# Score matmuls of the node slots in three bursts instead of four, the exponent scores first, on one ring of three bank pairs

## What is computed

```
for c in range(6):                       # nodes[-1] is the layer's input
    q = ew[c,0] * (nodes[in_q] @ We[eq] + be[eq])
    k = ew[c,1] * (nodes[in_k] @ We[ek] + be[ek])
    v = ew[c,2] * (nodes[in_v] @ We[ev] + be[ev])
    attn = softmax(heads(q @ Wq[c]) @ heads(k @ Wk[c]).T / sqrt(16))
    nodes[c] = act_w[c] * (attn @ heads(v @ Wv[c])) @ Wo[c] + q
out = layernorm(nodes[5])
```

## Time and profile before

| | |
|---|---|
| median of 3 runs | 1158.76 us (1156.9 to 1162.1) |
| profiled execution: its time, its span | 1160.02 us, 1158.2 us |
| mean granted clock of TensorE | 0.987 of full speed |
| busy share of PE, DVE, ACT, POOL | 96%, 72%, 64%, 37% |
| weight loads (PEld) | 67% |

### The profile page before, as it was taken

One profiled execution on the slowest core, in us unless ns is written; L12 is line 12 of the kernel. 1 busy time (PEld: TensorE's weight loads), 2 busy tenths in 40 slices (PEclk: granted clock), 3 DMA queues, 4 the chain that ended last, 5 costly groups with the idle time before them and its releaser, 6 DMA issues.

```text
span 1158.2 us, 28158 instructions
## 1 busy us (share of the span) xinstructions
PE 1114.4 (96%) x10313; PEld 774.3 (67%) x10313; DVE 836.6 (72%) x1857; ACT 738.9 (64%) x1597; POOL 428.4 (37%) x848
## 2 busy tenths in 40 slices
PE   8989999988999999999999999999999999999995
PEld 3755555555777777777777777677777777777773
DVE  5467888767787777777777788777777777777783
ACT  3345665553666766676666677666766766666674
POOL 3211121123333333333333488533333333333475
PEclk9789999999999999999999999999999999999998
DMA  8000000027665666666666676766666656666540
GB/s 226 1 1 1 1 0 0 1 36 97 91 84 84 93 93 93 86 87 96 93 90 84 87 101 102 104 93 86 88 96 93 90 84 94 94 92 86 84 72 24
DMA packets 83549, 87.02 MB, mean 75 GB/s; under 512 B 11482, under 2 KB 69342, under 8 KB 83422
## 3 DMA queue, kind: packets, MB, share of 16 engines
q1 hardware_dynamic: 81774, 83.17, 49.5%
q0 software_dynamic: 848, 2.11, 1.1%
q10 hardware_dynamic: 800, 0.05, 0.0%
HBM read 6.51 MB, written 2.10 MB: 7 GB/s over the span
## 4 chain that ended last, share of the span: by engine, by line
PE 79%; POOL 6%; DVE 6%; issue 4%; ACT 3%; DMA 1%; ACTq 0%; SPq 0%; POOLq 0%; DVEq 0%
PE bank L1166 71%; PE bank L1519 3%; PE bank L1526 3%; PE bank L1492 1%; DVE region L958 1%; POOL hl L542 1%; POOL region L530 1%; DVE region L992 1%; DMA cols<-in_L_attn_gnorm_w 1%; DVE region L1079 1%; POOL out L600 1%; POOL region L427 1%; POOL xall L429 1%; POOL region L425 1%; POOL region L525 1%
## 5 line engine op out<-in xcount | busy, mean ns | idle before, releaser
L755 ACT ACTIVATE region<-bank 128x512 f32<-128x512 f32 x768 | 416.9, 595 | 262.3 <-PE bank L1166 250.2
L1079 DVE TENSOR_REDUCE region<-bank 128x2 f32<-128x512 f32 x768 | 491.9, 681 | 78.4 <-PE bank L1166 78.1
L1166 PE MATMUL bank<-st 48*128 48x256 f32 x3072 | 374.4, 351 | 2.5 <-DVE region L1079 1.7
L1166 PEld LDWEIGHTS bank<-st 48*128 48x128 f32 x3072 | 265.7, 189 | 81.2 <-issue 29.7
L1166 PE MATMUL bank<-region 128*32 128x256 f32 (+5 forms) x3586 | 256.9, 376 | 2.9 <-DVE region L918 1.1
L542 POOL TENSOR_TENSOR hl<-qk,one_col 128x512 fp32r<-128x512 f32 x96 | 99.9, 1040 | 404.9 <-ACT qk L720 404.9
L1166 PEld LDWEIGHTS bank<-region 128*32 128x32 f32 (+3 forms) x3586 | 129.1, 114 | 90.9 <-issue 23.2
L1166 PE MATMUL bank<-mst,ones 64*128 64x512 bf16 x768 | 150.6, 388 | 0.2 <-ACT region L755 0.2
L545 POOL TENSOR_TENSOR hl<-qk,hl 128x512 fp32r<-128x512 f32 x96 | 122.6, 1277 | 7.5
L1095 DVE COPY mrows<-bank 24x256 bf16<-24x256 bf16 x96 | 26.8, 279 | 98.7 <-PE bank L1492 98.5
L1087 DVE COPY region<-bank 128x512 f32<-128x512 f32 x96 | 64.2, 669 | 2.7 <-PE bank L1166 2.7
(11 more groups left out here) (196 smaller groups left out, 1451.5 us busy)
## 6 DMA issues: line engine op xcount, KB each, us to landing
st<-hl SPq DMA_DIRECT2D x576, 128.0 KB, 4.5
mst<-mrows SPq DMA_DIRECT2D x192, 6.0 KB
out<-xall POOLq DMA_DIRECT2D x15, 128.0 KB, 3.8
xall<-in_L_attn_hidden_states SPq DMA_DIRECT2D x1, 768.0 KB, 8.9
cst<-in_constants SPq DMA_DIRECT2D x1, 514.5 KB, 4.1
xT<-in_L_ffn_Wq SPq DMA_DIRECT2D x1, 384.0 KB
xT<-in_L_ffn_Wk SPq DMA_DIRECT2D x1, 384.0 KB
xT<-in_L_ffn_Wv SPq DMA_DIRECT2D x1, 384.0 KB
```

What stands on the lines that cost most here:

```text
L755: act.activation(to, x_bank(x, k, e)[:, :].rearrange("p (j q) -> p j q", j=2), ACT.Exp).then_inc(B["exp_ok"], 1)
L1079: dve.tensor_reduce(mx[s.n % 2][:, to:to + 2], s_bank(s, k, e)[:, :].rearrange("p (j k) -> p j k", j=2), AX_X, ALU.max, negate=True).then_ ...
L1166: return pe.matmul(o, w, x, start=start, stop=stop, skip_group_check=skip)
```

## The change

PE issues the score work of a slot in three bursts: weights(0), scores(0), scores(1); then weights(1), weights(2), scores(2); then weights(3), scores(3). Both kinds draw bank pairs from one ring of three, and `banks_free` waits for whoever held the pair three places before. `project_v` moves up to where `project_qk` stood, and `project_qk` moves down behind `transpose_ctx`. On DVE `maxes(s, 1)` goes ahead of `copy_rows` and `maxes(s, 2)` ahead of `normalise`. On ACT `copy_vals` follows `exps(x, 2)`, `exps(x, 3)` is cut around `copy_ctxT`, and `copy_qk` comes last. On POOL `split_maxima` works on the step whose maxima have just been taken, at the end of the slot instead of at the start of the next, ahead of `split(a)` and behind the final layer norm.

```diff
-S_RING, X_RING = (0, 1, 2), (4, 5, 6)
+FIRST_RING = (0, 1, 2)
+RING = ((4, 5), (0, 1), (2, 6))
+ORDER = (("x", 0), ("s", 0), ("s", 1), ("x", 1), ("x", 2), ("s", 2), ("x", 3), ("s", 3))
...
 # POOL
             def phase(t, a, s, m, x, d, z, w):
-                if m is not None:
-                    split_maxima(m)
...
+                if s is not None:
+                    split_maxima(s)
                 if a is not None:
                     split(a)
...
 # ACT
+                if x is not None:
+                    exps(x, 2)
+                if m is not None:
+                    copy_vals(m)
                 if z is not None and z.last:
                     inverse_root(fve, fr, z.f, "fve_ok", "frl", "fra", B)
+                if x is not None:
+                    exps(x, 3, (0,))
+                if d is not None:
+                    copy_ctxT(d)
+                if x is not None:
+                    exps(x, 3, (1,))
                 if a is not None:
                     copy_qk(a)
-                if x is not None:
-                    exps(x, 2)
-                if d is not None:
-                    copy_ctxT(d)
-                if m is not None:
-                    copy_vals(m)
-                if x is not None:
-                    exps(x, 3)
...
 # DVE
+                if s is not None:
+                    maxes(s, 1)
                 if m is not None:
                     copy_rows(m)
                 if d is not None:
                     copy_raw(d)
                 if s is not None:
-                    maxes(s, 1)
+                    maxes(s, 2)
                 if d is not None:
                     normalise(d)
                 if s is not None:
-                    maxes(s, 2)
                     maxes(s, 3)
...
 # PE
+            def banks_free(t, kind, k, e):
+                old = holder(place(t, kind, k))
+                if old is None and t == EARLY:
+                    pe.wait_ge(B["max_ok"], UNITS)
+                elif old is None:
+                    pe.wait_ge(A["x1_ok"], ITERS)
+                elif old[0] == "s":
+                    pe.wait_ge(B["max_ok"], old[1] + e + 1)
+                else:
+                    pe.wait_ge(B["exp_ok"], old[1] + e + 1)
...
-                burst(0)
+                burst((0,), (0, 1))
...
-                burst(1)
+                burst((1, 2), (2,))
...
-                if a is not None:
-                    project_qk(a)
+                if m is not None:
+                    project_v(m)
                 if d is not None:
                     transpose_raw(d)
-                burst(2)
+                burst((3,), (3,))
...
                 if d is not None:
                     transpose_ctx(d)
-                if m is not None:
-                    project_v(m, a)
-                burst(3)
+                if a is not None:
+                    project_qk(a)
                 if d is not None:
                     project(d)
```

More of the change, by code:

```diff
@@ L376, in stages, with place, holder @@
             return (t, *(at_slot(t, n) for n in (0, S_AT, M_AT, X_AT, D_AT, Z_AT, W_AT)))
+        def place(t, kind, k):
+            return t * len(ORDER) + ORDER.index((kind, k))
+        def holder(p):
+            for q in range(p - len(RING), EARLY * len(ORDER) - 1, -len(RING)):
+                kind, k = ORDER[q % len(ORDER)]
+                n = at_slot(q // len(ORDER), S_AT if kind == "s" else X_AT)
+                if n is not None:
+                    return kind, n.n * UNITS + 2 * k
+            return None
         def s_bank(s, k, e):
-            return bank[S_RING[(s.n * UNITS + 2 * k + e) % len(S_RING)]]
+            if s.n + S_AT < EARLY:
+                return bank[FIRST_RING[(2 * k + e) % len(FIRST_RING)]]
+            return bank[RING[place(s.n + S_AT, "s", k) % len(RING)][e]]
         def x_bank(x, k, e):
-            return bank[X_RING[(x.n * UNITS + 2 * k + e) % len(X_RING)]]
+            return bank[RING[place(x.n + X_AT, "x", k) % len(RING)][e]]
         def unit(k):
@@ L608, in _ @@
             for t in range(1, EARLY):
-                phase(*stages(t))
+                split(stages(t)[1])
+            split_maxima(stages(EARLY - 1)[2])
             node_slots(phase)
@@ L743, in later_weights, with exps @@
                     transposed_weights(c)
-            def exps(x, k):
+            def exps(x, k, halves=(0, 1)):
                 g, kt = unit(k)
-                for e in range(2):
+                for e in halves:
                     u = x.n * UNITS + 2 * k + e
@@ L1449, in scores @@
                     pe.wait_ge(stacked[r], 96 * s.uses(STACKS))
-                for e in range(2):
-                    before = s.n * UNITS + 2 * k + e - len(S_RING)
-                    if before >= 0:
-                        pe.wait_ge(B["max_ok"], before + 1)
+                if s.n + S_AT < EARLY:
+                    if 2 * k + 1 >= len(FIRST_RING):
+                        pe.wait_ge(B["max_ok"], 2 * k + 2 - len(FIRST_RING))
+                else:
+                    for e in range(2):
+                        banks_free(s.n + S_AT, "s", k, e)
                 for n in range(2):
@@ L1466, in weights @@
                     pe.wait_ge(m_in[x.n % 2], 32 * x.uses(2))
-                if x.n == 0 and k == 0:
-                    pe.wait_ge(A["x1_ok"], ITERS)
                 for e in range(2):
                     rows = slice(HALF * e, HALF * e + HALF)
-                    before = x.n * UNITS + 2 * k + e - len(X_RING)
-                    if before >= 0:
-                        pe.wait_ge(B["exp_ok"], before + 1)
+                    banks_free(x.n + X_AT, "x", k, e)
                     mm(x_bank(x, k, e)[:, :].rearrange("p (j q) -> p j q", j=2), ones[rows, :], mst[x.n % 2][rows, 2 * g:2 * g + 2, :], stop=False, skip=True)
@@ L1481, in weights, with in_free @@
                             i.then_inc(B["x_ps"], 1)
+            def in_free(m):
+                if m.n + M_AT <= STEPS:
+                    pe.wait_ge(B["qk_ok"], m.n + M_AT)
+                else:
+                    pe.wait_ge(B["vals_ok"], m.n)
             def transpose_maxima(m):
                 pe.wait_ge(B["mlo_ok"], m.n + 1)
-                if m.n > 0:
-                    pe.wait_ge(B["vals_ok"], m.n)
-                else:
-                    pe.wait_ge(B["qk_ok"], M_AT)
+                in_free(m)
                 to = bank[IN][0:MCOLS, 0:P].bitcast(BF16)
@@ L1542, in phase, with burst @@
             def phase(t, a, s, m, x, d, z, w):
-                def burst(k):
+                def burst(xs, ss):
+                    if x is not None:
+                        for k in xs:
+                            weights(x, k)
                     if s is not None:
-                        scores(s, k)
-                    if x is not None:
-                        weights(x, k)
-                burst(0)
+                        for k in ss:
+                            scores(s, k)
+                burst((0,), (0, 1))
                 if t - 2 in TAILS:
-                    pe.wait_ge(B["vals_ok"], m.n)
+                    in_free(m)
                     transpose_x1(TAILS[t - 2], IN)
```

15 lines of the change are left out of this document (4 added, 11 removed).

## The result

The changed kernel takes 1192.91 us (median, 1191.7 to 1194.84), the kernel before 1159.49 beside it: the ratio is 1.028, 95% interval 1.0259 to 1.0299. The change costs 33 us. The forecast was slower, but 1168, with 1183 as the upper end.

The account below looks back on a forecast made before the run. PE bounded the kernel at 8.99 us a slot; after the change the key transfers' loop would, at 9.11. 80 x 0.12 = +9.6, +1 for final-norm slots and -2.5 at the ends, on 1158.8, gave 1168 us; range 1146 to 1183.

Parts of the forecast that it names:

- the price of a changeover: On PE, entering a burst with the shifts first costs 0.09 us, not 0.20; shifts end 0.32 after `project`.
- the sum: Adding up the ends in a slot: PE alone needs 8.28 us, with DVE's lateness 8.51, against 8.99 before.
- DVE's stall: `normalise` on DVE ends late, so PE stalls 0.23 us at `transpose_ctx` and `project_qk` ends at 7.66.
- the transfers decide: Keys from the late `project_qk` land at 18.41 us, for scores two slots on; this sets the slot at 9.08, taken as 9.11.
- Copy and split: From `project_qk`'s end to the first key transfer's issue, on ACT and POOL: 2.13 us, plus 0 to 0.1 for `split_maxima`.
- The rest is one slack-free loop: Scores(0) end 0.55 us after the keys land and 0.80 into the slot, so 2T + 0.80 = 18.96, T = 9.08.
- The second rival: Maxima rows land with the keys, so weights(0) starts 0.8 us late: T 9.21, time 1176 us; chance 0.12.
- The first two slots and the last five: These slots do not wait for transfers and win by fewer changeovers: -2.5 us, 0.3 to 0.5 each.
- The +1 for the final-norm slots: Slots with a final norm are bound by POOL, same work in another order: +1 us, bounds 0 and +9.
- +9.6: The 80 normal slots each take 0.12 us more, 9.11 against 8.99.
- the gap ahead of `transpose_ctx`: A sign to be seen on PE: a gap of 0.2 us there, ended by a DVE operation.
- The gap: A sign: PE idles about 0.6 us between weights(0) and the first scores, ended by a transfer; before weights(0) means forecast wrong.

Follow-up runs that it names:

- e6: The changed kernel with four key transfers a set instead of six from the sixth step on (stale data remain): 1128.7 us, ratio 0.971.
- e4: The kernel before, with weights ahead of scores inside each of its four bursts: 1135.99 us, ratio 0.9791.
- e3: The changed kernel with `project_qk`, `project_v` and their copies back in their old places, and POOL's split ahead of `split_maxima`: 1138.45 us, ratio 0.9806.
- e5: The kernel of e3 with POOL's order as in the change, `split_maxima` ahead of the split of keys: 1211.95 us, ratio 1.0449.
- e2: The kernel before, with only `project_v` and `project_qk` (and their copies on ACT) exchanged: 1180.81 us, ratio 1.0182.
- e7: The kernel of e3 with the context's transposes ahead of the third burst: 1130.99 us, ratio 0.973 to the kernel before.
- e1: The changed kernel with the two transfers of the maxima rows issued by POOL instead of SP: 1264.31 us, ratio 1.0905.
- e9: The kernel of e7 with eight filler matmuls ahead of the second burst of the first node slot: 1126.68 us, ratio 0.9711.
- e8: The changed kernel with eight filler matmuls ahead of the second burst of the first node slot: 1194.4 us, ratio 1.029.

## Why the prediction was wrong

**Right: the price of a changeover.** In the slot that doesn't wait the first shifts end 0.33 after `project` (909.59 to 909.92), forecast 0.32. PE with only DVE late gives 8.51 by the sum; it is 8.49 in the slots that don't wait, and 8.49 throughout in e6. e4 isolates the order inside the burst. DVE's stall was forecast as 0.23, and the wait of `transpose_ctx`'s weight loads for L1125 is 21.2 us over 84 times, 0.25 each.

**Right: the transfers decide, and the terms of their time.** Issue to landing was taken as 8.58 and 0.05 to notice, 8.63; it measures 8.60. From the first shifts to the end of `project_qk` the sum has 7.73 (7.66, and they start 0.07 before `project`'s end); it measures 7.69. Copy and split were 2.13 plus 0 to 0.1; it is 2.29, as `split_maxima` costs 0.16.

**Wrong: what the landing holds up.** The step that failed is "The rest is one slack-free loop. Scores(0) end 0.55 after the landing", that is, that only the keys' own readers wait for the set. The rows land with it, and they hold up weights(0), which starts 0.07 before the slot's zero, while scores(0) end at 0.80. With the forecast's own terms the loop through weights(0) is 2T = 7.73 + 2.17 + 8.63 = 18.53, T = 9.27, which is the measured 9.28. The loop through scores(0) gives 9.08. The price of that one edge is 0.19 a slot, 15 us in 80 slots.

**The second rival was the right mechanism with the wrong price.** It said that rows landing with the keys start weights(0) late, and gave it 0.12. Its 9.21 came from adding to the forecast's slot 0.8 less the idle time and dividing by two. The lateness was taken within the slot as forecast, when it is a loop of its own and has to be closed again, from release to release. Closed, it gives 1180 instead of 1176 (80 x 0.28 = 22.4, +1 and -2.5, on 1158.8). The rows shown ahead of the prediction could not decide it, as the maxima rows went out 2 us after the sixth transfer there. But the trace of the kernel before could, by its semaphore increments: the set issued from 600.47 on has its last at 609.08, and the rows issued from 605.76 on at 608.87; from 300 to 1100 us the rows' last lies, in eight pairs of ten, within 0.21 before and 0.26 after the set's. And with the set issued as late as the sum had it, the answer to this question was worth 0.19 a slot, and the case should have had far more than 0.12.

**Wrong: the first slots.** "The first two slots and the last five ... win by fewer changeovers: -2.5". The first three lose 7.2, and the last four, with a final norm among them, 1.8. In the first three slots there is no steady overlap: three waits of 1.58, 1.87 and 3.17 us stand there, and PE's clock goes down behind the first two and again behind the third. e4, with the ring, the bursts' number and POOL's order of before, loses nothing there (23.9); e3, with three bursts and keys early, loses 3; e5, with only POOL's order added to that, loses the 7. So, counted in this order, POOL's order holds 4 of the 7 and the three bursts with their ring 3 (e2 shows that the exchange of the projections, alone, costs 3 too). How these add up together, and how much of each is the low clock, isn't settled. The term of -2.5 had neither these waits nor the clock in it. The +1 for the final-norm slots was of the right size: 0.8 for t = 46 to 53.

Taken together: forecast +9.6, +1 and -2.5 make +8; measured +24.1, +0.8, and +7.2 and +1.8 at the ends, with -0.5 outside the slots, make +33.3 (rounded). Of the 25 us missed, 14.5 are normal slots, which is the loop that was closed through the wrong reader, and 11.5 the ends.

**Of the signs named beforehand**, PE's busy share (8.4 of 9.28 us), the gap ahead of `transpose_ctx` and the unchanged landing time came. The gap was said to stand after weights(0), and stands before it, which had been named as the sign that the forecast is wrong.

## What to carry to other kernels

A step moved later in a software-pipelined slot takes all transfers behind it along; follow them to every reader of anything that lands with them, not only to the reader of the moved data, and close the loop from release to release for each reader before pricing it. On an engine with few instructions, look at what stands ahead of the moved step there: exchanging two operations of POOL was worth 73 us here, while PE's reordering gave 22 to 31 (e3, e4, e7). The gain was in the part that moved nothing (e4, two lines), and the start-up and special slots of a pipeline need a sum of their own, as their waits are whole microseconds.

## What the runs showed of the hardware

- Small transfers (6 KB) issued while six of 128 KB are under way land with those, on another queue as well: 4.4 us (median) after issue in e1. With no set under way they landed 1.2 us after their issue ended, once 1.5 (five cases in e4, e6, e7, e9). In the kernel before they land with the set too (608.87 and 609.08), and no instruction waits for them.
- With the bf16 matmuls (64 rows) first, the change from full-array to row-tiled matmuls costs 0.12 us less than with the 48-row fp32 ones first: 0.79 against 0.91 for the burst (e4), in the same number of matmuls.
- After 4 us with 1.02 us of matmuls the granted clock was 0.55 to 0.60 for the next 8 us, and matmuls took 0.80 instead of 0.50. A filler for a gap of 1.87 us left the low clock as large as it was in one kernel (e8) and moved and halved it in another (e9, 1.2 us gained).
